# Two experts of a token by a search for the largest values, in place of counting those above each

## What is computed

```
t = _rmsnorm(x, g2).reshape(-1, D)                 # layer 1
probs = jax.nn.softmax(t @ router_w, axis=-1)      # 8 values a token
vals, idx = jax.lax.top_k(probs, K)                # K = 2
w = vals / jnp.sum(vals, axis=-1, keepdims=True)
...
xf = xn.reshape(-1, d)                             # layer 2
logits = xf @ Wg.T + bg
probs = jax.nn.softmax(logits, axis=-1)
tp, ti = jax.lax.top_k(probs, K)
tp = tp / (jnp.sum(tp, axis=-1, keepdims=True) + EPS_TOPK)
```

## Time and profile before

| | |
|---|---|
| time, median of 3 runs | 2389.68 us (2386.49 to 2404.02) |
| the profiled execution's own time | 2409.28 us |
| its span | 2407.4 us, mean granted PE clock 0.813 |
| busy PE, DVE, ACT, POOL | 1726.3 (72%), 1379.3 (57%), 953.7 (40%), 751.6 (31%) |
| DVE, gating of all 16 groups | about 90 us |

### The profile page before, as it was taken

How to read it: one execution, slowest core, us unless ns; L and a number is a source line. 1 busy time by engine, 2 the same in 40 slices (tenths; PEclk the granted TensorE clock), 3 DMA queues, 4 the chain that set the end, 5 groups by cost and what they waited for, 6 DMA issues and landing times. The chain is left out here.

```text
span 2407.4 us, 42348 instructions
## 1 busy us (share of the span) xinstructions
PE 1726.3 (72%) x14895; PEld 1218.7 (51%) x14902; DVE 1379.3 (57%) x4069; ACT 953.7 (40%) x1904; POOL 751.6 (31%) x1131
## 2 busy tenths in 40 slices
PE   2668879999688888898977874673681397874323
PEld 1335547667466666454544663552441386763211
DVE  4556664442477676475665445443864523658666
ACT  3335443333256665453433442341440264642112
POOL 4322100100522221234332116215516402253663
PEclk9868889999799888897888897786665598996555
DMA  6536555300255454221211122543530222120100
GB/s 176 119 78 125 105 178 156 70 1 1 44 113 103 92 99 77 87 49 46 52 48 52 40 66 66 124 105 125 121 71 32 78 64 69 63 71 27 35 27 9
DMA packets 189757, 184.46 MB, mean 77 GB/s; under 512 B 29509, under 2 KB 177925, under 8 KB 183557
## 3 DMA queue, kind: packets, MB, share of 16 engines
q1 hardware_dynamic: 180540, 145.04, 26.1%
q10 hardware_dynamic: 816, 19.92, 2.7%
q0 software_dynamic: 8192, 16.79, 2.4%
HBM read 119.47 MB, written 80.74 MB: 83 GB/s over the span
## 5 line engine op out<-in xcount | busy, mean ns | idle before, releaser
L2067 DVE TENSOR_REDUCE mneg<-psb 128x4 f32<-128x512 f32 (+1 forms) x576 | 386.6, 685 | 242.1 <-PE psb L1678 206.2
L2457 ACT ACTIVATE HB<-psb 128x512 f32<-128x512 f32 x384 | 222.3, 596 | 228.6 <-PE psb L1678 193.9
L1678 PE MATMUL psb<-K,Q 96*128 96x128 bf16 x1280 | 188.3, 249 | 66.2 <-DVE mneg L2067 27.2
L2677 POOL TENSOR_SCALAR rs<-mv 128x2 f32<-128x2 f32 (+1 forms) x96 | 22.7, 237 | 663.8 <-DVE mv L2027 655.3
L2457 ACT ACTIVATE HB<-psb,bias 128x512 f32<-128x512 f32 x192 | 131.5, 685 | 204.6 <-PE psb L1678 168.8
L1678 PE MATMUL psb<-Q,K 99*128 99x128 bf16 x1280 | 146.7, 246 | 88.3 <-DMA Q<-mT 87.1
L1678 PEld LDWEIGHTS psb<-K,Q 96*128 96x128 bf16 x1280 | 112.0, 111 | 122.5 <-issue 55.3
L1678 PEld LDWEIGHTS psb<-Q,K 99*128 99x128 bf16 x1280 | 108.6, 112 | 123.1 <-issue 108.4
L1678 PE MATMUL psb<-HB,VA 128*9 128x128 f32 (+1 forms) x2560 | 149.8, 313 | 13.0 <-issue 9.6
L1678 PE MATMUL psb<-KS,Q 96*128 96x128 bf16 x1024 | 150.0, 237 | 12.0 <-DVE mneg L2067 11.9
L1678 PE MATMUL psb<-K 128*128 128x256 f32 x576 | 152.7, 411 | 3.6 <-issue 2.6
(11 more groups left out here) (432 smaller groups left out, 4049.5 us busy)
## 6 DMA issues: line engine op xcount, KB each, us to landing
tok_rows<-in_zero ACTq DMA_DIRECT2D x16, 1152.0 KB, 31.1
K<-sc_k SPq DMA_DIRECT2D x32, 384.0 KB, 5.1
Q<-sc_q SPq DMA_DIRECT2D x32, 384.0 KB
sc_q<-comp SPq DMA_DIRECT2D x48, 192.0 KB, 2.2
K<-tok_rows SPq DMA_DIRECT2D x72, 128.0 KB
y_rows<-K SPq DMA_DIRECT2D x72, 128.0 KB
sc_q<-comp SPq DMA_DIRECT2D x48, 128.0 KB, 2.1
vraw<-in_ctx SPq DMA_DIRECT2D x48, 128.0 KB, 6.8
```

Source lines behind the costliest of these rows:

```text
L1678: return pe.e.matmul(out, w, x, start=start, stop=stop, skip_group_check=True)
L2067: t = e.tensor_reduce(m.mneg[:, s.b % 4, s.i * A.per:(s.i + 1) * A.per], PSB[s.use.bank].rearrange("p (h k) -> p h k", h=A.per), AX.X, ALU ...
L2457: a.done(act(m.HB[:, s.slot, :], PSB[s.use.bank], ACT.Exp, bias=bz), s.use.drained)
L2677: then(e.tensor_scalar(r0, var, EPS, None, ALU.add))
```

## The change

The logits of a token are searched by two DVE instructions: `max` writes the 8 largest of a row in falling order, `max_index` their indices. Each takes one row of 8 values a partition, so a group of 4 sequences needs four of each. `LG` becomes twice as wide: the logits in columns 0 to 7, the sorted ones in 8 to 15. One subtraction takes the largest off all 16 and writes them to a new tile `EG`, whose exponentials ACT takes at once; `max_index` stands behind the subtraction on DVE. The weights come from columns 8 and 9 of `EG`, in E2 with the sum of the 8 exponentials times 1e-8, and one multiplication by the reciprocal. The comparison of pairs, its scratch in `AT` and the wait for that scratch are gone, and with them the step gate_rank; of its costs and gate_pick's the planner's table now says 1600 in all, and gate_logits stands with 1900 on PE and 2200 on DVE in place of 300 and 650. The step gate_pick now waits for the group before to be placed. PE's matmuls for place wait for `pickb`, the fourth of the instructions of gate_pick, and no longer for its ninth.

```diff
-        "gate_logits": lambda: (("pe", 300), ("dve", 650)),
+        "gate_logits": lambda: (("pe", 1900), ("dve", 2200)),
-        "gate_rank": lambda: (("dve", 2600),),
-        "gate_pick": lambda: (("dve", 2800),),
+        "gate_pick": lambda: (("dve", 1600),),
...
     def gate_logits(s):
...
-        v.wait_ge(v.step(e.tensor_reduce(s0, L, AX.X, ALU.max)))
-        v.done(e.tensor_tensor(L, L, wide(s0), ALU.subtract), s.done)
+        for j in range(4):
+            t = e.max(V[:, j, :], L[:, j, :])
+        v.wait_ge(v.step(t))
+        v.done(e.tensor_tensor(E, m.LG[:, s.g % 2], V[:, :, 0:1].broadcast_to([128, 4, 16]), ALU.subtract), s.done)
+        for j in range(4):
+            t = e.max_index(ix[:, j, :], V[:, j, :], L[:, j, :])
+        v.step(t)
+
+    def gate_pick(s):
+        bs = slice(4 * s.g, 4 * s.g + 4)
+        E, ix, s0, s1 = m.EG[:, s.g % 2], m.ix[:, s.g % 2], m.small[:, 0, bs], m.small[:, 1, bs]
+        M, ek = m.pick, m.ek[:, s.i, :, bs]
+        v.wait_ge((v.chain, v.n), s.need)
+        t = v.step(e.tensor_copy(ek.rearrange("p k b -> p b k"), ix[:, :, 0:2]))
+        t2 = v.step(e.tensor_tensor(s0, E[:, :, 8], E[:, :, 9], ALU.add))
+        v.wait_ge(t)
+        number = C("blocks")[:, 0:8].unsqueeze(1).unsqueeze(1).broadcast_to([128, 2, 4, 8])
+        v.wait_ge(v.step(e.tensor_tensor(M[:, :, :, :], number, ek.unsqueeze(3).broadcast_to([128, 2, 4, 8]), ALU.is_equal)))
+        v.done(e.tensor_tensor(m.pickb[:, :, :], M[:, 0], M[:, 1], ALU.add), s.done)
+        if s.plus:
+            v.wait_ge(v.step(e.tensor_reduce(s1, E[:, :, 0:8], AX.X, ALU.add)))
+            v.wait_ge(v.step(e.scalar_tensor_tensor(out=s0, in0=s1, scalar=s.plus, in1=s0, op0=ALU.mult, op1=ALU.add)))
         v.wait_ge(v.step(e.reciprocal(s1, s0)))
+        v.step(e.scalar_tensor_tensor(out=m.gk[:, s.i, :, bs].rearrange("p k b -> p b k"), in0=E[:, :, 8:10], scalar=1.0,
+                                      in1=s1.unsqueeze(2).broadcast_to([128, 4, 2]), op0=ALU.mult, op1=ALU.mult))
```

More of the change, by code:

```diff
@@ L10 @@
 I32 = mybir.dt.int32
+U32 = mybir.dt.uint32
 F32R = mybir.dt.float32r
@@ L374, in __init__ @@
         self.oT = sb("oT", [128, 2, 128])
-        self.LG = sb("LG", [128, 2, 4, 8])
-        self.GT = sb("GT", [128, 2, 4, 8])
+        self.LG = sb("LG", [128, 2, 4, 16])
+        self.EG = sb("EG", [128, 2, 4, 16])
+        self.ix = sb("ix", [128, 2, 4, 8], U32)
         self.small = sb("small", [128, 3, 32])
@@ L1231, in n6 @@
                 return False
-            do("gate_rank", g=g, big=E.big, need=got["t"], free=E.begin, done=inc("dve", "ranked"))
-        def n7():
             got["k"] = inc("dve", "picked")
-            do("gate_pick", g=g, i=E.i, big=E.big, plus=E.plus, done=got["k"])
+            do("gate_pick", g=g, i=E.i, plus=E.plus, gi=E.gi, need=(got["t"], t_tg), done=got["k"])
         def n8():
@@ L1253, in n9 @@
                 E.end(h)
-        return [*([n0] if E.i else []), n1, n2, n3, n4, n5, n6, n7, n8, *[(lambda j=j: n9(j), lambda: got["p"]) for j in range(4)]]
+        return [*([n0] if E.i else []), n1, n2, n3, n4, n5, n6, n8, *[(lambda j=j: n9(j), lambda: got["p"]) for j in range(4)]]
     def blocks(E, h, t_w, start, bank):
@@ L2139, in f1_end @@
         v.done(e.tensor_tensor(u, PSB[s.use.bank][:, 0:128], u, ALU.add), s.use.drained)
[L2141 to L2150, removed]
     def gate_logits(s):
-        _, L, T, s0, s1 = gate_views(s.g)
+        L, V, E, ix = m.LG[:, s.g % 2, :, 0:8], m.LG[:, s.g % 2, :, 8:16], m.EG[:, s.g % 2], m.ix[:, s.g % 2]
         P3 = PSB[s.use.bank][:, 0:32].rearrange("p (b e) -> p b e", b=4)
@@ L2160, in gate_logits @@
         v.wait_ge(v.done(t, s.use.drained))
-        v.wait_ge(v.step(e.tensor_reduce(s0, L, AX.X, ALU.max)))
-        v.done(e.tensor_tensor(L, L, wide(s0), ALU.subtract), s.done)
[L2164 to L2168, removed]
-        v.wait_ge(v.step(e.reciprocal(s1, s0)))
[L2170 to L2199, removed]
@@ L2404, in vector_program @@
         sums_turn=sums_turn, x_add_otmp=x_add_otmp, x1_end=x1_end, halves=halves, w3s_scale=w3s_scale, f0_up=f0_up, f0_add=f0_add, f1_qk=f1_qk,
-        f1_end=f1_end, gate_logits=gate_logits, gate_rank=gate_rank, gate_pick=gate_pick, place=place, block_table=block_table, y_index=y_index,
+        f1_end=f1_end, gate_logits=gate_logits, gate_pick=gate_pick, place=place, block_table=block_table, y_index=y_index,
         block_gate=block_gate, block_down=block_down, combine=combine, q_load=q_load, len_sums=len_sums, q_abs=q_abs, q_scale=q_scale,
@@ L2509, in gate_exp @@
     def gate_exp(s):
-        L = m.LG[:, s.g % 2]
+        E = m.EG[:, s.g % 2]
         a.wait_ge(s.need)
-        a.done(act(L, L, ACT.Exp), s.done)
+        a.done(act(E, E, ACT.Exp), s.done)
     def table(s, kind, most):
```

4 lines of the change are left out of this document (2 added, 2 removed).

## The result

The changed kernel takes 2383.74 us (median of 18 runs) where the kernel before takes 2398.15 (18 runs). Three later timings gave 0.992, 0.990 and 0.992, with intervals of about 0.003 to each side. Forecast were 29 us. The profiled executions differ by 19.6 us (spans 2407.4 and 2387.8).

What follows compares the result with a forecast made beforehand. PE was taken to bound full-clock AF stretches, a group-to-group chain with POOL's 13.6 us period the end of A2. Terms -23, -2 and -4 made -29 us: 2380.6 profiled, 2361 as median from 2389.7, range 2338 to 2388.

Steps and rivals of the forecast that it cites:

- Term 1: End of A2 and what follows: shorter gates and earlier groups bring -23 us (-13 to -24).
- (c): End of A2: POOL sets periods of 13.6 us, four from norm g3 to norm g7, with 2.0 us to spare.
- (d): End of A2: g7's way to `pidx` takes 10.9 us instead of 13.4, ending at 1874.4 instead of 1897.07.
- (b): End of A2: g3's statistics stand behind the closing of 1804.06, so its norm comes at 1809.1 instead of 1825.55.
- (a): End of A2: g1's scatter, its place behind the closing at 1789.54, starts at about 1793.4 and ends at 1803.5.
- What is behind (table, loads, blocks) has the same order and follows `pidx`: Behind g7's `pidx`: block table, loads and blocks keep their order and follow it; no separate cost was given.
- Term 2: E2's g0: POOL waits 31.77 us for its `pidx`; the shorter gate counts in part, -2 us (0 to -4).
- Term 3: E1's groups beside AF: PE hides DVE's 22 us, split scatters can take away an ACT stall; -4 us (-20 to +15).
- (B): Rival, chance 0.17: the order gives back +5 to +15 us beside AF against -15 to -23 at the end; 2370 to 2390.
- (C): Rival, chance 0.15: E1 gains too, two stalls go and DVE's relief counts, -12 to -25 us more; 2336 to 2350.
- (D): Rival, chance 0.10: end groups come no sooner, g1's place waits for PE's counts; 2373, or 2377 with dear searches.
- (A): Rival, chance 0.08: searches are dear, 1 us each, a group takes 10 us; +28 to +39 us, 2418 to 2429.

Runs made afterwards that it cites:

- old_ops_new_order: The kernel before's comparison of pairs with the changed kernel's order (rank and pick one step, new table numbers); 1.0067 of the kernel before.
- old_new_again: Same program as old_ops_new_order, timed and profiled again in the series where the kernel before takes 2304 us; 1.0106 of the kernel before.
- no_index: Changed kernel in its order without `max_index`: logits compared with the two largest, numbers by product and sum behind the weights; 0.9892 of the kernel before.
- best: Changed kernel with E1's gates planned as before, E2's as changed, and no `max_index`; 0.9914 of the kernel before.
- searches_twice: Changed kernel in its order with each `max` and each `max_index` issued twice; 0.9913 of the kernel before.
- tiles_last: Changed kernel with the tiles `EG` and `ix` allocated behind all others; 0.9911 of the kernel before, table 13.2 us.
- code_shifted: Changed kernel with 72 short memsets more at the start of DVE's program; table 11.8 us, no whole time given.
- old_ops_with_index: old_ops_new_order with four `max_index` a group whose results nobody reads; AF 366.9 us, table 8.0 us, no whole time given.
- new_ops_old_order: Changed kernel's searches with the order of before, gate_rank a step of its own and old table numbers; 0.9993 of the kernel before.

## Why the prediction was off

The mechanism at the end of A2 was right and nearly of the size; the sum was 12 us too large, from several places.

**The gate itself** was right. 42 us of DVE were forecast, 41.3 measured; the searches cost 0.96 us a group instead of 1.2, logits and pick of g7 2.7 (1867.42 to 1868.83 and 1868.87 to 1870.18) instead of 3.3. The rule that the next operation waits until the pipe is empty (the Trainium skill, VectorE: DVE Perf Modes, section The DRAIN you can't avoid) would have made 8 searches 1.4 us; here four `max` of 0.155 us each are done within 0.37. The same section of the Trainium skill adds that an operation that is not held starts earlier, and the trace agrees with that, with starts 0.07 to 0.09 us apart: the prediction took the rule without its exception. The Trainium skill, Vector Engine (DVE) Microarchitecture Reference, section 3.9, says that positions come from a separate pass of a load and a search; the trace agrees, and the load costs only 0.07 us.

**Term 1**, -23, measured -19.9 from the same matmul at A2's end. Steps (c) and (d) hold: periods of 13.6 us without a wait, and 10.1 us from norm g7 to its places (forecast 10.9). Step (b), the norm of g3 straight behind the closing before last, holds as a chain, too. Of the 2.8 us that are missing (22.7 against 19.9) 1.5 lie in the base: the forecast was worked out from the first profile of before, in which this stretch took 112.2 us, and in the two others it took 110. The other 1.3 come from the norm of g3, which was to start 20.8 us behind the matmul of A2's end (1805.7 against 1784.92) and started 22.6 to 24.3 us behind it; the periods and g7's way gave 1.0 us back. What failed is that steps (a) and (b) took the attention's last closings to come as before and priced nothing for PE's late counts: ACT stood 7.9 us, and the closings that g3's statistics wait for came no earlier against g0's places. In old_ops_new_order such a wait costs 6 us against the same program without it. The scatter is not enough to make it, since in old_new_again it stands at the same place. In the series at about 2400 us all eleven profiles with E2's new order have the wait there, and none of the five with E2's old order, in which g1's scatter starts 15 to 17 us behind the matmul instead of 6 to 9. So it takes the new order and something that the faster series lacked; what, stays open.

**"What is behind (table, loads, blocks) has the same order and follows `pidx`"** is the step that failed outright. The order is the same, and yet the table takes 9.5 to 13.0 us in the four profiles of the changed kernel instead of 8.0, 4.5 us by the stretches. What the runs show in its place is that DVE's counts on itself come late between the table's operations. `no_index` and `best`, with tables of 8.7 and 8.3 us, point to `max_index`; `searches_twice`, with twice as many of them and a table of 8.0, shows that its presence is not enough. `tiles_last` speaks against the tiles' addresses, `code_shifted` against the place of the code, each with one profile. `old_ops_with_index` decides nothing, as it ran only where PE's late counts were gone as well. In 7 of 18 cases in the first profile the count comes within 0.12 us of the end of a POOL operation (DVE goes on at 1857.70, POOL's DMA instruction ends at 1857.74), in the others it does not, and kernels without searches have as much of POOL's work beside DVE's. The cause stays open.

**Term 2**, -2, measured -1.7 up to g0's places, and A2 gave it back with +2.0: what starts A2 is not g0's scatter alone.

**Term 3**, -4, measured -3 to -7: PE hides most of DVE's 21 us, as said. The size came right by luck, for the reason given, split scatters that take ACT's stalls away, was not it. ACT's waits with an unnamed releaser beside AF did shrink, from 47 to 52 us in the three profiles of before to 39 to 41 in the four of the changed kernel; but new_ops_old_order has 51 us of them and takes 385.3 us, and with short gates both orders take 385 to 389 us. Both rivals of this place missed as well. (B) has the right mechanism, an order that costs beside AF, but its cause is gates that PE meets too early: it needs the long gates, which the change has not. (C) wanted 12 to 25 us more beside AF, and they did not come. (D), that g1's places come no sooner, is refuted: its scatter starts 6 to 7 us behind the matmul of A2's end, where it started 15 to 17. In (A) the break-even of 0.7 us a search can't be read from a run; that gates of any length can cost beside AF is seen in `old_ops_with_index`, where 0.65 us more a gate cost 10 us in one profile.

**The sum.** -3, -2, +2, -20, +4.5 and +1 make -17.5, against 17 us by the ratio and 14.4 by the medians. The forecast for the time was 2361, the lower end of its range 2338, the upper 2388; the time lies in the range. Of the 23 us between forecast and time 8.5 are the base, which was 2389.7 as the median of 3 runs and is 2398.2 as that of 18.

## What to carry to other kernels

Where a chain from group to group sets the time, work out its period and that of each engine on it; the shorter gate was worth 2.5 us at the end and 7 with the waits it removed, and the same change with a planner's new order 20, some of it lost again at the next step of the chain. A table of costs has to be changed together with what it describes: the new numbers with the old operations cost 0.7 to 1.1% in the time, the new operations with the old numbers gained nothing that can be told from zero (0.1%). A kernel that is to rule out a cause has to run where the effect is seen: the one with `max_index` added ran only where the same program was 94 us faster and waits of another kind were gone, too. And a transfer that moves forward has to be charged with what it meets there, as it was not here.

## What the runs showed of the hardware

- `max` on 128 x 8 takes 0.155 us, and independent ones start 0.07 to 0.09 us apart; `max_index` is a load of 0.07 us and a search of 0.16, one pair every 0.14 us.
- DVE's counts on its own semaphore can come up to 1.3 us late (code_shifted, behind the cast of `pidx` in the table), in a stretch of one program and in every profile of it: some 6 to 21 times in the kernels with `max_index` in the place of the comparison, 1 to 3 with `max` alone, never with the comparison.
- PE's counts for ACT can come 3 to 7 us after the modelled end of the matmul (3.0, 5.4 and 5.9 us in the changed kernel near 1795, 6.6 in old_ops_new_order near 1806). ACT's waits with an unnamed releaser, in which these show, make up 119 to 132 us of the kernel before in three profiles and 3.7 us in two others.
- The same program took 2304 us in one series and 2395 to 2402 in the five others; beside AF 330 us at a granted clock of 0.97 against 390 to 403 at 0.86 to 0.89. The granted clock is not all of it, as ACT's waits above show.
